# Attention with gated experts on one core: weighted sums in pairs, row statistics issued by POOL, and a context chunk ahead of the third stack loads

## Chip, cores and metric

One core of a Trainium2 chip (trn2) runs the whole program. The metric is device time in microseconds (us), median of the runs, lower is better. Engines: PE is TensorE, ACT ScalarE, DVE VectorE, POOL GpSimd, SP SyncE, which here only issues DMAs.

## What is computed

x is 8 x 512 x 256 float32, the context 8 x 1601 x 256. Cross-attention with 16 heads of 16 channels and a gated residual come first, then a feed-forward over 8 experts of which each token takes two. The softmax of the attention runs over the queries (axis 2 of head, query, key), so each key row is normalised on its own:

```python
def _L0_xattn_ref(q, k, v, Wq, Wk, Wv, Wo):
    scale = Dm ** (-0.5)
    qh, kh, vh = heads(q @ Wq.T), heads(k @ Wk.T), heads(v @ Wv.T)
    attn = jnp.einsum('bhnc,bhlc->bhnl', qh * scale, kh)
    attn = jax.nn.softmax(attn, axis=2)
    attn = attn / jnp.sum(attn, axis=-1, keepdims=True)
    out = jnp.einsum('bhnl,bhlc->bhnc', attn, vh)
    return out @ Wo.T

x = x + jnp.tanh(g_xattn[0]) * _L0_xattn_ref(_layernorm(x), ctx_1024, ctx_1024, Wq, Wk, Wv, Wo)
x = x + jnp.tanh(g_ffn[0]) * _L0_ffn_ref(_layernorm(x), router_w, w1, w2)   # 8 experts, top 2, exact gelu
```

## The kernel before, in words

**The attention loop.** The 8 batches follow one another, each in 52 steps: 4 groups of 4 heads, by 13 tiles of 128 key rows (12 whole ones, and a 13th of the 64 rows that are left; the single last key row is handled apart, as "lone" row). A step is: scores of the tile for the 4 heads, in two units of two heads each (`unit_scores`, PE, two matmuls of 128x512, L822); for each unit the negated maximum over the queries (DVE, L1247); exp with the sum as a by-product, one activation per head (ACT, L1041); the reciprocal of the sums (DVE, L1231); the value rows scaled by it (POOL, `weigh_values`, L1469); and, LAG = 3 steps later, the weighted sum of the tile into the accumulator `acc` (`weigh`, PE, L849: 8 matmul records, four of them side by side in 32 columns each). The lone row's sum (L855) hangs behind the `weigh` of one step in each group (steps 12, 15, 34 and 47 in batches 1 to 7; 12, 25, 38 and 51 in batch 0).

**Two rings.** Scores live in 3 PSUM slots, one a unit. The matmul of head j of unit u waits for the activation of the same head of unit u - 3 (L821). So the first unit of step s+1 waits for the second unit of step s-1. Probabilities live in a ring of 4 steps: ACT's first activation of step s waits for `weigh` of step s-4 (L1038).

**Side work.** `FILL_AT` gives single steps a "fill" of the one bank `spare`: the projections of the next batch (k in 8 pieces, q in 2, v in 7), turns (transposes) of the outputs of this batch, and the output projection, logits and prefix sums of the batch before. A k, q or v piece (not the last v) and an output projection are halved: the first half on PE in the step before, the second in its own step (`Iteration.halves`). ACT takes a k or q piece at the start of its step (L983), DVE the residual (L1134), POOL two more bf16 parts (L1533 and, a step later, L1525), and SP stores the parts to DRAM (`store_parts`, L502). From there SP loads them as the stacks of the next batch (`load_stacks`, 16 DMAs a group, L459 and L464).

**PE's order** is written out in `run` of the tensor block (L859 to L879). In a plain step: first unit, fill, second unit, then `weigh` of step s-3. Where `begins_behind(s)` holds (a first half or a turn begins in s, and s-1 had a fill too, and step s-3 isn't the first of its group), `weigh` of s-3 comes right behind the first unit instead.

**Row statistics of the next batch.** DVE makes mean and variance by step 16 (L1280), POOL the reciprocal deviation in step 17 (`one_over_deviation`, L1439 and L1441). SP then writes both to DRAM as 2 x 512 single float32 (`spread_x_stats`, L514), waits for that to land (L518), and reads them back onto all partitions (`gather_x_stats`, L519). POOL uses them in steps 24 to 27 (L1514, L1518). In batch 0 these two stand in SP's order before the stores of k pieces 3 and 4, in the others behind the store of piece 4.

**Context.** `load_ctx` (L526, L531) loads the context of batch b+2 in 4 column chunks at the end of an iteration, behind the stack loads of groups 1 and 2; chunk c waits for the v piece that reads its columns last. Piece 0 of k in the next iteration, whose first half is in step 0, reads chunk 0 (L740).

After the last batch come routing and 71 blocks of expert work, which the change leaves alone.

Of the kernel before, what the change touches and what calls it, by code (L numbers as in the profile page):

```python
# [33 lines left out]
P = 128  # L34
# [7 lines left out]
KC = D // P  # L42
# [18 lines left out]
KCHUNK = 4  # L61
# [91 lines left out]
SHIFT_X = 24  # L153


class Iteration:
# [32 lines left out]
    def begins_behind(self, s):  # L189

        begun = any(halves == (0,) or f[0] in TURNS for f, halves in self.halves(s))
        return begun and self.fill(s - 1) is not None and (s - LAG) % GROUP_STEPS > 0
# [62 lines left out]
def attention_and_routing(nc, ctx, block, keep, x, x_t_in, ctx_t, g_xattn, g_ffn, wq_t, wk_t, wv_t, wo_t, router_t,  # L255
# [236 lines left out]
    def _(sp):  # L492
# [17 lines left out]
        def spread_x_stats(it):  # L510
            b = it.b
            sp.wait_ge(rstd_step, 2 * (b + 2))
            for s, stat in ((0, mv1[:, :, 0]), (1, rstd1[:, 1, :])):
                sp.dma_start(x_stats_dram[s].rearrange("(t p) -> p t", p=P), stat, allow_slow_non_contiguous=True).then_inc(x_stats_stored, 16)  # L514

        def gather_x_stats(it):
            b = it.b
            wait_apart(sp, x_stats_stored, 32 * (b + 1), passed_sp)  # L518
            sp.dma_start(x_stats[:, :, :], x_stats_dram.partition_broadcast(P)).then_inc(x_stats_in, 16)  # L519

# [5 lines left out]
        def load_ctx(it):  # L526

            for c in range(KCHUNK):
# [29 lines left out]
        def run(it):  # L558
# [13 lines left out]
            if it.next:  # L572
# [3 lines left out]
                for c in ORDER[0:KCHUNK]:  # L576
                    if b == 0 and c == KC + 3:
                        spread_x_stats(it)
                    store_parts(it, c)
# [3 lines left out]
            if it.next:  # L583
                for c in ORDER[KCHUNK:2 * KCHUNK]:
                    if b == 0 and c == KC + 4:
                        gather_x_stats(it)
                    store_parts(it, c)
                    if b > 0 and c == KC + 4:
                        spread_x_stats(it)
                        gather_x_stats(it)  # L590
# [10 lines left out]
            if it.next:  # L601
# [11 lines left out]
                for g in range(1, G - 1):  # L613
                    sp.wait_ge(scores_ready, units_by_group(b, g + 1))
                    load_stacks(b + 1, g)
            if it.ahead:
                load_ctx(it)
# [40 lines left out]
    def _(pe):  # L658
# [200 lines left out]
        def run(it):  # L859
            for s in range(STEPS):  # L860
                late = s >= LAG and it.cur and it.begins_behind(s)
                if it.cur:
                    unit_scores(it.b, s, 0)
                if late:
                    weigh(it.b, s - LAG)
                    if not it.fill(s):
                        unit_scores(it.b, s, 1)
                for f, halves in it.halves(s):
                    fill(it, *f, halves)
                if late and it.fill(s):  # L870
                    unit_scores(it.b, s, 1)
                if it.tail and s == LOGITS - 1:
                    first_logits(it)
                if it.cur and not late:
                    unit_scores(it.b, s, 1)
                    if s >= LAG:
                        weigh(it.b, s - LAG)
# [961 lines left out]
```

## Time and profile before

| | us |
|---|---|
| median of 3 runs (lowest to highest) | 1807.41 (1803.83 to 1809.83) |
| the profiled execution's own time | 1806.2 |
| its span, first to last instruction | 1804.5 |
| mean granted TensorE clock | 0.994 of full speed |

The profiled execution lies 1.2 us below the median; between its span and its own time lie 1.7 us. In the rows below a line is: start (us from the span's start), duration, engine (PEld is PE's weight load, SPq and POOLq a DMA queue), line of the kernel, operation, output tile <- input tiles, shapes, number of records merged into the row, and in brackets how long the engine had been idle before it and who ended that. A row of the waits is: who waited for whom, us in total, times, longest. w_all is the tile that holds stacks, context and probabilities, room holds x, attention output and statistics. An iteration's work on all five engines runs side by side, so an idle time counts only where nothing else covers it.

### The profile page before, as it was taken

How to read it: one execution, taken by the hardware profiler on the slowest of the kernel's cores; microseconds unless marked ns; L12 is line 12 of the kernel's file. 1: busy time of each engine (PE TensorE's matmuls, PEld its weight loads, DVE VectorE, ACT ScalarE, POOL GpSimd, SP SyncE). 2: the span in 40 equal slices, each digit the busy share in tenths (PEclk: the TensorE clock that was granted, in tenths of full speed). 3: DMA queues.
4: the chain of work that ended last, by engine and by line, in shares of the span. 5: the costliest groups of instructions: out<-in, count | busy, mean ns of one | idle time of the engine just before them, and what ended most of it. 6: DMA issues, size and time to landing. Idle time of an engine off the chain costs nothing.

```text
span 1804.5 us, 32470 instructions
## 1 busy us (share of the span) xinstructions
PE 1706.4 (95%) x10342; PEld 925.6 (51%) x10466; DVE 1399.6 (78%) x2320; ACT 1250.0 (69%) x3521; POOL 550.6 (31%) x830
## 2 busy tenths in 40 slices
PE   8989899999999999999999999889899999999997
PEld 5223333333333333333233333225899999999997
DVE  7978899999899999999989999997344444444442
ACT  5989899999999999999999999996111111111111
POOL 3231153343234234334323522213222222222222
PEclk9999999999999999999999999999999999999999
DMA  8638514712821651481282154319322222222221
GB/s 227 151 61 204 131 49 123 211 40 67 227 71 52 180 152 45 123 215 41 66 222 77 47 147 121 137 71 270 117 38 35 38 35 35 38 35 38 35 36 29
DMA packets 144265, 182.12 MB, mean 101 GB/s; under 512 B 22448, under 2 KB 120880, under 8 KB 144144
## 3 DMA queue, kind: packets, MB, share of 16 engines
q1 hardware_dynamic: 129168, 159.67, 33.2%
q0 software_dynamic: 14144, 20.47, 6.5%
q8 instruction: 57, 0.93, 0.2%
q14 instruction: 64, 0.52, 0.1%
q10 hardware_dynamic: 832, 0.53, 0.1%
HBM read 126.69 MB, written 53.91 MB: 100 GB/s over the span
## 4 chain that ended last, share of the span: by engine, by line
PE 49%; DVE 26%; issue 9%; ACT 9%; DMA 3%; POOL 2%; SPq 2%; POOLq 0%; DVEq 0%; ACTq 0%
DVE negmax L1247 18%; PE scores L1651 14%; PE scores L1664 13%; ACT w_all L1041 8%; PE acc L849 7%; PE scores L822 6%; PE spare L686 3%; SPq L464 1%; DVE resid L1134 1%; PE acc L855 1%; DVE rz L1231 1%; DMA routed<-routed_rows,place 1%; PE spare L1641 1%; PE spare L672 1%; DVE o_acc L1237 1%
## 5 line engine op out<-in xcount | busy, mean ns | idle before, releaser
L1041 ACT ACTIVATE w_all<-scores,negmax 128x512 f32<-128x512 f32 x1600 | 1086.2, 749 | 57.1 <-DVE negmax L1247 53.1
L1247 DVE TENSOR_REDUCE negmax<-scores 128x2 f32<-128x1024 f32 x809 | 967.6, 1206 | 55.7 <-PE scores L822 47.0
L822 PE MATMUL scores<-q_stack,w_all 128*128 128x512 bf16 x1412 | 455.4, 384 | 54.5 <-ACT w_all L1041 37.7
L849 PE MATMUL acc<-w_all,vz 128*32 128x512 f32 x3328 | 443.7, 605 | 0.2
L1041 ACT ACTIVATION_READ_ACCUMULATOR w_all<-scores,negmax 128x1 f32 x1600 | 429.0, 268 | 0.0
L1697 ACT ACTIVATE projections<-scores 128x512 f32<-128x512 f32 x142 | 84.8, 597 | 446.8 <-PE scores L1651 441.7
L822 PEld LDWEIGHTS scores<-q_stack,w_all 128*128 128x128 bf16 x1536 | 129.3, 98 | 515.4 <-ACT w_all L1041 443.2
L1469 POOL TENSOR_TENSOR vz<-w_all,rz 128x68 f32<-128x68 f32 x416 | 124.7, 300 | 768.6 <-DVE rz L1231 728.2
L1651 PEld LDWEIGHTS scores<-row_t,q_stack 128*128 128x128 f32 x2272 | 264.5, 192 | 6.1 <-DVE row_t L1724 1.5
L1651 PE MATMUL scores<-row_t,q_stack 128*128 128x128 f32 x2272 | 265.6, 275 | 1.1 <-DVE row_t L1724 1.0
L1664 PE MATMUL scores<-room,projections 128*128 128x256 f32 x1136 | 256.8, 379 | 0.0
L1777 POOL DMA_INDIRECT out<-row_t,gate_token x71 | 118.7, 1671 | 410.8 <-DVE row_t L1737 376.9
L1664 PEld LDWEIGHTS scores<-room,projections 128*128 128x128 f32 x1136 | 210.4, 190 | 25.7
L1730 DVE COPY gate_token<-parts 128x2 f32<-128x2 f32 x71 | 12.0, 170 | 184.1 <-DMA out<-row_t,gate_token 184.1
L849 PEld LDWEIGHTS acc<-w_all,vz 128*32 128x32 f32 x3328 | 66.8, 108 | 136.9 <-issue 120.6
L1737 DVE TENSOR_SCALAR row_t<-scores,gate_token 128x256 f32<-128x256 f32 x71 | 34.4, 484 | 96.5 <-PE scores L1664 96.4
L672 PE MATMUL spare<-w_all,projections 128*128 128x409 f32 (+1 forms) x228 | 98.5, 515 | 7.2 <-DMA w_all<-in_ctx_t 3.8
L686 PE MATMUL spare<-projections,w_all 128*128 128x256 f32 x400 | 104.5, 384 | 0.3 <-ACT w_all L968 0.2
L1714 DVE COPY q_stack<-w_all 128x2048 f32 x71 | 87.0, 1226 | 1.5 <-issue 1.5
L1719 DVE COPY room<-w_all 128x2048 f32 x71 | 86.4, 1217 | 0.0
L686 PEld LDWEIGHTS spare<-projections,w_all 128*128 128x128 f32 x400 | 75.8, 192 | 16.7 <-issue 3.5
L1231 DVE RECIPROCAL rz<-z 128x4 f32<-128x4 f32 x416 | 69.8, 168 | 6.3 <-ACT w_all L1041 6.3
(231 smaller groups left out, 1162.1 us busy)
## 6 DMA issues: line engine op xcount, KB each, us to landing
w_all<-k_parts SPq DMA_DIRECT2D x248, 204.4 KB, 3.7
w_all<-in_w SPq DMA_DIRECT2D x16, 1024.0 KB, 10.2
q_stack<-q_parts SPq DMA_DIRECT2D x248, 64.0 KB, 3.5
k_parts<-parts SPq DMA_DIRECT2D x42, 306.8 KB, 3.4
w_all<-in_ctx_t SPq DMA_DIRECT2D x24, 409.0 KB, 6.5
parts<-routed SPq DMA_DIRECT2D x71, 129.0 KB
q_parts<-parts SPq DMA_DIRECT2D x14, 384.0 KB, 3.9
routed<-pad_row SPq DMA_DIRECT2D x8, 645.0 KB
```

The lines of the kernel that those rows point to most:

```text
L672: mm = pe.matmul(bank[:, 0:KCOLS[c + 1] - KCOLS[c]], wk_sb[:, k, m * P:(m + 1) * P], ctx_sb[:, k, KCOLS[c]:KCOLS[c + 1]], start=(k == 0), ...
L686: mm = pe.matmul(bank[:, cols], rows, wv_sb[:, k, :], start=(k == 0), stop=(k == KC - 1))
L822: mm = pe.matmul(scores[:, bank + j % 2, :], k_stacks[g][:, j, lt * P:(lt + 1) * P], q_stack[:, g, j, :], start=True, stop=True)
L849: mm = pe.matmul(acc[32 * j:32 * j + 32, :], vz[:, s % RING, j, :], probs[:, s % RING, j if lt < LT else j // 2, :], start=(lt == 0), stop ...
L1041: act.activation(lone_probs[:, :] if alone else probs[:, s % RING, j, :], scores[:, 2 * (u % SLOTS) + j % 2, :], ACT.Exp, bias=negmax[:, u ...
L1231: dve.reciprocal(into, sums).then_inc(rz_ready, 1)
L1247: dve.tensor_reduce(negmax[:, u % 4, 0:n], scores[:, 2 * (u % SLOTS):2 * (u % SLOTS) + n, :], AX.X, ALU.max, negate=True).then_inc(negmax_ ...
L1469: pool.tensor_tensor(vz[:, s % RING, :, 0:DH + 1], v_ones[b % 2][:, lt, g * GH:(g + 1) * GH, :], rz[:, s % RING, :].unsqueeze(2).to_broadc ...
L1651: mm = pe.matmul(ps_hidden[:, slot * BANKS + h // HB, (h % HB) * BLK:(h % HB + 1) * BLK], w1_sb[:, slot, k * HID + h * P:k * HID + (h + 1) ...
L1664: mm = pe.matmul(ps_y[:, slot, 0:D], hidden[:, slot, h * BLK:(h + 1) * BLK], w2_sb[:, slot, h * D:(h + 1) * D], start=(h == 0), stop=(h == ...
L1714: dve.tensor_copy(w1_sb[:, slot, :], w1_all[:, bass.ds(e * (KC * HID), KC * HID)]).then_inc(w1_ready, 1)
L1777: pool.indirect_dma_start(out=out, out_offset=bass.IndirectOffsetOnAxis(gate_token[:, slot, 1:2].bitcast(U32), 0), in_=result[:, slot, :], ...
```

## The change

PE's order comes from a plan made per iteration (`weighed`). A `weigh` that would stand at the end of a step is put off where the next step has its own `weigh` behind the first unit: then both stand there, back to back. SP no longer issues the statistics: POOL issues the two stores in step 17, and in step 22 it waits for them and issues the read. The first context chunk is issued behind the stack loads of group 1, ahead of those of group 2.

```diff
--- before.py
+++ after.py
@@ -150,7 +150,7 @@
 OUT = 9
 STATS_X = (7, 11, 12, 13)
 CENTRE_X = 17
-SHIFT_X = 24
+SPREAD_X, SHIFT_X = 22, 24
 
 
 class Iteration:
@@ -189,7 +189,21 @@
     def begins_behind(self, s):
 
         begun = any(halves == (0,) or f[0] in TURNS for f, halves in self.halves(s))
-        return begun and self.fill(s - 1) is not None and (s - LAG) % GROUP_STEPS > 0
+        return begun and self.fill(s - 1) is not None
+
+    def weighed(self):
+
+        plan, following = [], 0
+        for s in range(STEPS):
+            due = s - LAG
+            behind, at_end = range(0), range(0)
+            if following <= due:
+                if self.begins_behind(s) and due % GROUP_STEPS > 0:
+                    behind, following = range(following, due + 1), due + 1
+                elif not (s + 1 < STEPS and self.begins_behind(s + 1) and (due + 1) % GROUP_STEPS > 0):
+                    at_end, following = range(following, due + 1), due + 1
+            plan.append((behind, at_end))
+        return plan
 
     def chunk(self, name, i):
 
@@ -507,25 +521,14 @@
                 load_q_block(sp, stack_in[g], b, g, blk)
                 load_k_block(sp, stack_in[g], b, g, blk)
 
-        def spread_x_stats(it):
-            b = it.b
-            sp.wait_ge(rstd_step, 2 * (b + 2))
-            for s, stat in ((0, mv1[:, :, 0]), (1, rstd1[:, 1, :])):
-                sp.dma_start(x_stats_dram[s].rearrange("(t p) -> p t", p=P), stat, allow_slow_non_contiguous=True).then_inc(x_stats_stored, 16)
-
-        def gather_x_stats(it):
-            b = it.b
-            wait_apart(sp, x_stats_stored, 32 * (b + 1), passed_sp)
-            sp.dma_start(x_stats[:, :, :], x_stats_dram.partition_broadcast(P)).then_inc(x_stats_in, 16)
-
         def load_x(it):
 
             sp.wait_ge(xn_ready, 2 * (it.b + 2))
             sp.dma_start(x_in[:, :, :], x_rows[it.b + 2]).then_inc(x_loaded, 16)
 
-        def load_ctx(it):
-
-            for c in range(KCHUNK):
+        def load_ctx(it, chunks):
+
+            for c in chunks:
                 cols = slice(KCOLS[c], KCOLS[c + 1])
                 sp.wait_ge(fill_taken, it.made("v", last_v_of(c)))
                 sp.dma_start(ctx_sb[:, :, cols], ctx_rows[it.b + 2][:, :, cols]).then_inc(ctx_in[c], 16)
@@ -574,20 +577,13 @@
                 for g in range(G):
                     wait(sp, stack_in[g], stacks_by(b, g))
                 for c in ORDER[0:KCHUNK]:
-                    if b == 0 and c == KC + 3:
-                        spread_x_stats(it)
                     store_parts(it, c)
             if it.tail:
                 sp.wait_ge(fill_taken, it.made("out_proj", 1))
                 sp.dma_start(out_rows[b - 1], x2[:, :, :]).then_inc(x2_stored, 16)
             if it.next:
                 for c in ORDER[KCHUNK:2 * KCHUNK]:
-                    if b == 0 and c == KC + 4:
-                        gather_x_stats(it)
                     store_parts(it, c)
-                    if b > 0 and c == KC + 4:
-                        spread_x_stats(it)
-                        gather_x_stats(it)
             if b == 0:
                 load_stacks(0, 3)
             if it.cur:
@@ -613,8 +609,10 @@
                 for g in range(1, G - 1):
                     sp.wait_ge(scores_ready, units_by_group(b, g + 1))
                     load_stacks(b + 1, g)
+                    if g == 1 and it.ahead:
+                        load_ctx(it, range(1))
             if it.ahead:
-                load_ctx(it)
+                load_ctx(it, range(1, KCHUNK))
 
         def load_w1_behind(group):
 
@@ -857,24 +855,21 @@
             mm.then_inc(pv_done, 1)
 
         def run(it):
-            for s in range(STEPS):
-                late = s >= LAG and it.cur and it.begins_behind(s)
+            for s, (behind, at_end) in enumerate(it.weighed()):
                 if it.cur:
                     unit_scores(it.b, s, 0)
-                if late:
-                    weigh(it.b, s - LAG)
-                    if not it.fill(s):
-                        unit_scores(it.b, s, 1)
+                for step in behind:
+                    weigh(it.b, step)
+                if behind and not it.fill(s):
+                    unit_scores(it.b, s, 1)
                 for f, halves in it.halves(s):
                     fill(it, *f, halves)
-                if late and it.fill(s):
-                    unit_scores(it.b, s, 1)
                 if it.tail and s == LOGITS - 1:
                     first_logits(it)
-                if it.cur and not late:
+                if not (behind and not it.fill(s)):
                     unit_scores(it.b, s, 1)
-                    if s >= LAG:
-                        weigh(it.b, s - LAG)
+                for step in at_end:
+                    weigh(it.b, step)
                 if s < LAG and it.tail:
                     weigh(it.b - 1, STEPS + s - LAG)
 
@@ -1506,6 +1501,12 @@
                 if it.next and s == CENTRE_X:
                     wait_apart(pool, mv_ready, (b + 2) * NT, passed_pool)
                     one_over_deviation(mv1, rstd1, rstd_step, (b + 1) * 2)
+                    for i, stat in ((0, mv1[:, :, 0]), (1, rstd1[:, 1, :])):
+                        pool.dma_start(x_stats_dram[i].rearrange("(t p) -> p t", p=P), stat,
+                                       allow_slow_non_contiguous=True).then_inc(x_stats_stored, 16)
+                if it.next and s == SPREAD_X:
+                    wait_apart(pool, x_stats_stored, 32 * (b + 1), passed_pool)
+                    pool.dma_start(x_stats[:, :, :], x_stats_dram.partition_broadcast(P)).then_inc(x_stats_in, 16)
                 if it.next and s in (SHIFT_X, SHIFT_X + 1):
                     k = s - SHIFT_X
                     if k == 0:
```

## Rows read from the trace of the kernel before

**Rows 1.** Page, busy time of each engine over the span.
```profile
PE 1706.4 (95%) x10342; PEld 925.6 (51%) x10466; DVE 1399.6 (78%) x2320; ACT 1250.0 (69%) x3521; POOL 550.6 (31%) x830
```

**Rows 2.** Timeline of batch 3, steps 13 to 15, engines PE, ACT and DVE.
```profile
536.16 0.38 PE L822 MATMUL scores<-q_stack,w_all 128*128 128x512 bf16 x1
536.47 1.06 PE L849 MATMUL acc<-w_all,vz 128*32 128x512 f32 x8
536.52 0.68 ACT L1041 ACTIVATE w_all<-scores,negmax 128x512 f32<-128x512 f32 x1
537.47 0.61 PE L822 MATMUL scores<-q_stack,w_all 128*128 128x512 bf16 x2
538.01 1.06 PE L849 MATMUL acc<-w_all,vz 128*32 128x512 f32 x8
538.89 1.04 PE L855 MATMUL acc<-lone_probs,lone_vz 128*17 128x512 f32 x8
539.86 0.61 PE L822 MATMUL scores<-q_stack,w_all 128*128 128x512 bf16 x2
...
540.51 1.22 DVE L1247 TENSOR_REDUCE negmax<-scores 128x2 f32<-128x1024 f32 x1 [0.63 <-PE scores L822]
541.77 0.69 ACT L1041 ACTIVATE w_all<-scores,negmax 128x512 f32<-128x512 f32 x1
```

**Rows 3.** Timeline of batch 3, steps 45 and 46, ACT and PE.
```profile
629.54 0.87 ACT L1041 ACTIVATE w_all<-scores,negmax 128x512 f32<-128x512 f32 x1
...
630.56 0.39 PE L822 MATMUL scores<-q_stack,w_all 128*128 128x512 bf16 x1 [0.24 <-ACT w_all L1041]
```

**Rows 4.** Timeline of batch 3, steps 35 to 37, ACT and PE.
```profile
602.77 0.83 ACT L1041 ACTIVATE w_all<-scores,negmax 128x512 f32<-128x512 f32 x1
...
606.12 0.66 PE L754 MATMUL spare<-ident,room 128*128 128x128 f32 x4
...
608.75 0.69 ACT L1041 ACTIVATE w_all<-scores,negmax 128x512 f32<-128x512 f32 x1 [0.56 <-DVE negmax L1247]
```

**Rows 5.** Timeline of batch 3, steps 6 to 8, ACT and PE.
```profile
516.41 0.71 ACT L1041 ACTIVATE w_all<-scores,negmax 128x512 f32<-128x512 f32 x1
...
518.78 0.61 PE L822 MATMUL scores<-q_stack,w_all 128*128 128x512 bf16 x2
```

**Rows 6.** Timeline, end of batch 0 to step 0 of batch 1, SP and PE.
```profile
185.17 2.12 SPq L531 DMA_DIRECT2D w_all<-in_ctx_t  x4
...
190.51 0.58 PE L672 MATMUL spare<-w_all,projections 128*128 128x408 f32 x1 [3.81 <-DMA w_all<-in_ctx_t]
```

**Rows 7.** Timeline, ACT: first activation and take of k piece 2, batches 1 and 3.
```profile
188.74 0.69 ACT L1041 ACTIVATE w_all<-scores,negmax 128x512 f32<-128x512 f32 x1
...
225.82 0.58 ACT L983 ACTIVATE parts<-spare 128x409 bf16<-128x409 f32 x1
...
497.06 0.69 ACT L1041 ACTIVATE w_all<-scores,negmax 128x512 f32<-128x512 f32 x1
...
528.02 0.58 ACT L983 ACTIVATE parts<-spare 128x409 bf16<-128x409 f32 x1
```

**Rows 8.** Waits of the SP queue: the stores of the statistics.
```profile
SPq L231 <- DMA x_stats<-rstd: 70.5, 7, 12.4
```

**Rows 9.** Timeline of batch 0, steps 17 to 24, POOL, SP and ACT.
```profile
85.58 0.96 POOL L1525 TENSOR_TENSOR parts<-resid,parts 128x409 bf16<-128x409 f32 x1
...
92.72 0.36 SPq L502 DMA_DIRECT2D k_parts<-parts  x1
...
103.63 0.52 ACT L983 ACTIVATE parts<-spare 128x409 bf16<-128x409 f32 x1 [4.26 <-DMA k_parts<-parts]
...
111.02 0.69 ACT L1041 ACTIVATE w_all<-scores,negmax 128x512 f32<-128x512 f32 x1 [2.87 <-DVE negmax L1247]
```

**Rows 10.** Stores of k parts in 60 to 130 us: landing times, minimum, median, maximum.
```profile
DMA to landing us min/median/max: 3.1/3.9/10.8
```

**Rows 11.** Timeline, start of the run, POOL issuing eight loads.
```profile
22.90 4.11 POOL L459 DMA_DIRECT2D q_stack<-q_parts  x8 [3.02 <-DMA q_parts<-w_all]
```

## The prediction

> **What bounds the kernel now.** I read the page first. PE is busy 95% of the span and DVE 78% [rows 1], but these are averages over two stages, and the change touches only the attention loop, so I went on to its timeline. There a step holds four activations on ACT, two maxima of 1.22 us on DVE [rows 2], and two units of scores, a weighted sum of about 1 us and the side work on PE. The three engines run at nearly the same rate, so the question in each step is whose chain ends last. Steps 13 to 15 of batch 3 show it [rows 2]: DVE stood idle for 0.63 us until the second unit of step 15 (539.86) was there, and ACT could begin that unit only at 541.77. PE spent the time before on two weighted sums and the lone row's. In step 37 ACT idles 0.56 us in the same way [rows 4]. Batches 2 to 6 repeat the pattern.
>
> Two stalls stand outside this rhythm. In batch 1, step 0, PE waits 3.81 us for the context's first chunk [rows 6]. In batch 0, step 23, ACT waits 4.26 us for a store of k parts, which landed 10.8 us after its issue at 92.72, where the median is 3.9 [rows 9, 10]; a wait of 2.87 us follows in step 25. In front of that store SP had issued the statistics, 2 KB a piece in single floats, which took up to 12.4 us to land [rows 8].
>
> **Part 1, weighted sums in pairs.** The plan makes 16 pairs in each of batches 1 to 6, 14 in batch 0 and 3 in batch 7, 113 in all. What a pair saves can be read: from one weighted sum to the scores behind it PE needs 1.00 us (536.47 to 537.47), to the lone row's sum behind it, which has the same column form, only 0.88 (538.01 to 538.89). Into a weighted sum it is 0.31 us from the last scores matmul (536.16 to 536.47), while a scores matmul takes 0.23 where nothing changes (537.47 to 538.01 for two, less the 0.31). So a pair saves about 0.12 + 0.08 = 0.20 us of PE [rows 2].
>
> What it costs is a cover. The first unit of step s+1 needs the slot that ACT's second unit of step s-1 leaves. Before, a weighted sum stood between, and hid that wait. Now PE waits with both sums still to do, and the second unit of step s+1 stands behind them. The latency from an activation's end to the matmul that waited for it is 629.54 + 0.87 = 630.41 to 630.56, so 0.15 us [rows 3]. With that each pair can be worked out.
>
> Steps 14/15: the slot's last activation ends at 536.52 + 0.68 = 537.20, so the second matmul of the unit starts at 537.35. Then 0.31 into the first sum, 0.88 to the second, 0.88 to the lone row's, 0.97 out of it (538.89 to 539.86): second unit at 540.39 instead of 539.86, 0.53 later [rows 2]. DVE was waiting for it, so all of it reaches ACT.
>
> Steps 36/37: 602.77 + 0.83 + 0.15 = 603.75, then 0.31 + 0.88 + 0.88 + 0.97 gives the turn at 606.79 instead of 606.12, 0.67 later, and ACT, idle there, follows [rows 4]. Steps 49/50 have the same pattern, also with a lone row and a turn: 0.66.
>
> Steps 7/8: 516.41 + 0.71 + 0.15 = 517.27, then 0.31 + 0.88 + 1.00 gives 519.46 instead of 518.78, 0.68 later [rows 5]. DVE is not idle here, its own queue covers about half. Steps 3/4 and 9/10 are alike; I take 0.27 for each of the three. Steps 21/22 and 39/40 give 0.15 each. In the stretch of v pieces (steps 43 to 48), of q pieces and at 27/28 the delays fit under ACT, which is never idle there: nothing, as long as ACT's queue is full; without that cover each would cost 0.3.
>
> A steady batch: 0.53 + 0.67 + 0.66 + 0.8 + 0.3 = 2.96 us, six of them 17.8. Batch 0, with one lone row in a pair, I put at 1.2, batch 7 at 0.6. Sum +19.6. Bounds: all 113 pairs on the path and no slot wait save 0.20 x 113 = 23; the 68 pairs outside the stretch of v, with 0.68 each, would cost 46. I stay by the pairs worked out one by one.
>
> Here a rule speaks for the change. The Trainium skill, "TensorEngine Tiling (Array Packing)", Key Properties, says that changing the tiling mode drains TensorE. The 0.12 and 0.08 us of [rows 2] agree with it. By that rule alone the pairs would be worth the 23 us of the bound.
>
> **Part 2, context chunk 0.** It moves ahead of 16 DMAs. SP needs 2.12 us for four, 0.53 each, so it goes out 8.5 us sooner, about 176.7 instead of 185.17, and with the 5.3 us that it took (185.17 to 190.51) it lands at 182. PE began to wait at 190.51 - 3.81 = 186.70 [rows 6]. In other batches it was in time. Worth: from ACT's first activation to the take of k piece 2, batch 1 needs 225.82 - 188.74 = 37.08 us, batch 3 528.02 - 497.06 = 30.96 [rows 7]. The difference, 6.1 us, holds the wait and what the slower PE clock behind it cost. Late next is chunk 1, out at about 185.7 and landing at 191. It is needed two steps after chunk 0, and a step is 30.96 / 11 = 2.8 us [rows 7], so at 192.3; a wait of 1 us at most. Group 2's loads and the last chunks go out 0.5 us later and have a group's time. So -6.1, between -3.8 and -6.5.
>
> **Part 3, the statistics.** SP is free of them, POOL gets three DMAs. Eight loads cost POOL 4.11 us [rows 11], 0.5 each; stores in single floats may take 1. In step 17 POOL's low part of the piece before stands behind them, and the value rows of step 17, which have two steps of slack. In step 22 POOL waits for the landing. Five steps of 2.8 us are 14 us, the landing took up to 12.4 [rows 8], with POOL's issue added about 14 too. If it is late by 1 or 2 us, what stands behind it are value rows that PE needs three steps on: nothing. If that cover were gone, each such us would count in seven batches.
>
> Batch 0 is another matter. The low part of k piece 2, at 85.58 now [rows 9], moves to about 87.5, its store to 88.5, which is behind the statistics and no longer before them. ACT takes piece 4, which needs that store landed, two steps before it came to piece 5 (103.63 - 4.26 = 99.4), at about 93.8. If single-float writes hold up what is written after them, as they held piece 3's store for 10.8 us, the stall of 4.26 and most of the 2.87, say 6.6 us together, goes, and one of about the same size comes two steps sooner. If POOL's queue is apart, all 6.6 us go. Bounds: -6.6 and +5. I take 0, by the row that is nearest, the store that was held.
>
> The Trainium skill, "Trainium Kernel Development and Optimization", Key Constraints, says that DMAs of SP, ACT and POOL run on the same 16 DMA engines and that another issuing engine saves only issue time. By it the hold-up stays, and the sum is the one I give.
>
> **Sum**, on the profiled execution's own time: 1806.2 + 19.6 - 6.1 + 0 = 1819.7, that is 1820. The median is 1.2 above that execution; I leave it there. What a measurement of this kernel can tell from no change is about 0.3%, 5.4 us.
>
> **Rivals.**
> A. *Not slower: the late second units are absorbed.* Place: steps 3 to 15, 36/37, 49/50. DVE's queue or ACT's hides them, or the first unit, which is now up to 0.4 us sooner, gives the time back. For it: DVE and ACT are busy nearly all the time. Against: the idle times of 0.63 and 0.56 us stand exactly behind these units. It decides if the two sums end within 0.3 us of their old place. Time: 1806.2 - 6.1 = 1800, or 1794 if the statistics' stall goes too. Chance 0.17.
> B. *Faster: PE's column form is the bound.* Of 16 pairs 9 lie where PE is late; 57 x 0.20 = 11 us: 1806 - 6 - 11 = 1789. Against: the slot wait above. Chance 0.06.
> C. *As forecast, but POOL's queue is apart*: 1820 - 6.6 = 1813. Chance 0.20.
> D. *The new hold-up is longer than the old*: piece 2's store lands at 103, ACT waits 9 us and loses some 2 behind it, where 6.6 were lost: 1824. Chance 0.15.
> My forecast, 1820, has 0.42, its own range 1813 to 1827.
>
> **How the numbers follow.** Faster (under 1802): B and over half of A, 0.16. Same (to 1812.8): the rest of A, nearly half of C, a little of the forecast, 0.21. Slower: 0.63. The range 1799 to 1829 leaves out B, the low end of A and the high end of D.
>
> **What would show it.** Part 1: in step 15 of batch 3 the two sums in a row and the second unit 0.5 us later against ACT's activations, PE's waits for ACT at L822 grown, and a steady batch 3 us longer. Part 2: no wait for in_ctx_t, and 31 us from first activation to piece 2 in batch 1. Part 3: ACT's wait for k_parts in batch 0 gone, or moved to piece 4. I am wrong if steady batches are not longer than now.

## The result: 1.25% slower, and the profile after

| | before | changed |
|---|---|---|
| median (lowest to highest) | 1805.62 (1802.64 to 1809.83), 4 runs | 1828.76 (1824.76 to 1830.42), 4 runs |
| profiled execution, its span | 1806.2, 1804.5 | 1824.76, 1823.0 |

The ratio is 1.0125, 95% interval 1.0108 to 1.0143, that is +22.6 us (19.5 to 25.8). The forecast was 1820, slower: the sign held, the size was short, and the median lies 0.24 us inside the upper end of the range, 1829, and outside the forecast's own 1813 to 1827. Below, the page after: the busy line, the chain's shares by engine, and four of the costliest groups (busy, mean ns | idle before it, and who ended it).

```profile
PE 1692.1 (93%) x10347; PEld 946.7 (52%) x10466; DVE 1397.9 (77%) x2320; ACT 1254.4 (69%) x3521; POOL 568.9 (31%) x851
...
PE 41%; DVE 25%; ACT 24%; issue 7%; DMA 1%; POOL 1%; SPq 0%; DVEq 0%; POOLq 0%; ACTq 0%
...
L1036 ACT ACTIVATE w_all<-scores,negmax 128x512 f32<-128x512 f32 x1600 | 1085.8, 737 | 70.9 <-DVE negmax L1242 67.6
L1242 DVE TENSOR_REDUCE negmax<-scores 128x2 f32<-128x1024 f32 x809 | 968.7, 1207 | 66.3 <-PE scores L820 56.0
L820 PE MATMUL scores<-q_stack,w_all 128*128 128x512 bf16 x1417 | 454.5, 384 | 99.4 <-ACT w_all L1036 85.6
L847 PE MATMUL acc<-w_all,vz 128*32 128x512 f32 x3328 | 419.4, 601 | 0.4 <-POOL vz L1464 0.4
```

PE is busy 14 us less than before [rows 1] and the kernel is longer. The weighted sums alone (L847, before L849) went from 443.7 to 419.4 us. So the saving in PE's work was real: 24.3 us on the sums, where 113 pairs at the 0.20 us of [rows 2] make 23. But PE's wait for ACT in front of the scores grew from 37.7 to 85.6 us, DVE's wait for scores from 47.0 to 56.0, and ACT's for DVE from 53.1 to 67.6. The engine got idler, which is what a lost cover looks like.

The same place as [rows 2], steps 14 and 15 of batch 3, in the timeline after:

```profile
541.12 0.68 ACT L1036 ACTIVATE w_all<-scores,negmax 128x512 f32<-128x512 f32 x1
...
541.94 0.39 PE L820 MATMUL scores<-q_stack,w_all 128*128 128x512 bf16 x1 [0.28 <-ACT w_all L1036]
542.26 1.92 PE L847 MATMUL acc<-w_all,vz 128*32 128x512 f32 x16
544.00 1.04 PE L853 MATMUL acc<-lone_probs,lone_vz 128*17 128x512 f32 x8
544.98 0.61 PE L820 MATMUL scores<-q_stack,w_all 128*128 128x512 bf16 x2
...
545.62 1.23 DVE L1242 TENSOR_REDUCE negmax<-scores 128x2 f32<-128x1024 f32 x1 [1.15 <-PE scores L820]
...
546.88 0.69 ACT L1036 ACTIVATE w_all<-scores,negmax 128x512 f32<-128x512 f32 x1 [0.57 <-DVE negmax L1242]
```

The slot's last activation ends at 541.80 and the matmul that waited starts at 541.94. Then come both sums in one record of 16, the lone row's, and the second unit 3.18 us after the slot was free (544.98 - 541.80). Before it was 2.66 (539.86 - 537.20): 0.52 more, where the forecast had 0.53. DVE's idle time before that unit grew from 0.63 to 1.15. Steps 36/37 likewise, to set beside [rows 4], where ACT idled 0.56:

```profile
609.31 0.39 PE L820 MATMUL scores<-q_stack,w_all 128*128 128x512 bf16 x1 [0.26 <-ACT w_all L1036]
609.63 1.92 PE L847 MATMUL acc<-w_all,vz 128*32 128x512 f32 x16
611.37 1.04 PE L853 MATMUL acc<-lone_probs,lone_vz 128*17 128x512 f32 x8
612.35 0.66 PE L752 MATMUL spare<-ident,room 128*128 128x128 f32 x4
...
614.97 0.69 ACT L1036 ACTIVATE w_all<-scores,negmax 128x512 f32<-128x512 f32 x1 [1.21 <-DVE negmax L1242]
```

A batch's length is read from ACT's first activation in it to the first of the next. For batch 3, before it is the first of [rows 7] for batch 3 and the line below:

```profile
648.16 0.69 ACT L1041 ACTIVATE w_all<-scores,negmax 128x512 f32<-128x512 f32 x1
```

that is 151.10; after:

```profile
500.79 0.69 ACT L1036 ACTIVATE w_all<-scores,negmax 128x512 f32<-128x512 f32 x1
...
655.18 0.69 ACT L1036 ACTIVATE w_all<-scores,negmax 128x512 f32<-128x512 f32 x1
```

154.39. Read in this way for every step, the first activation of a step is later, against the kernel before, by 0.23 more from step 5 on, 0.39 from 10, 0.21 from 12, 0.50 from 16, 0.19 from 23, 0.23 from 25, 0.65 from 38, 0.14 from 41 and 0.61 from 51. I call these "jumps" below; they add up to 3.15, and the other 0.14 of the 3.29 lies in shifts of under 0.1 us each. Batches 3 to 6 all have them (in batch 4 0.21 of the last comes at step 49 already). The others: batch 0 157.41 to 159.31, batch 1 157.22 to 154.88, batch 2 151.11 to 155.30, with 0.9 more than its neighbours at step 23, and batch 7, read to the start of its last step, 137.04 to 139.12.

The other two parts of the change, batch 0 on POOL and ACT, then the turn of the batch on SP:

```profile
85.18 0.85 POOL L1505 DMA_DIRECT2D x_stats<-mv  x1 [0.29 <-POOL rstd L1436]
86.02 0.77 POOL L1505 DMA_DIRECT2D x_stats<-rstd  x1
86.81 0.98 POOL L1526 TENSOR_TENSOR parts<-resid,parts 128x409 bf16<-128x409 f32 x1
...
99.39 0.51 ACT L978 ACTIVATE parts<-spare 128x408 bf16<-128x408 f32 x1 [6.38 <-DMA k_parts<-parts]
...
175.14 0.58 SPq L534 DMA_DIRECT2D w_all<-in_ctx_t  x1
...
186.74 1.61 SPq L534 DMA_DIRECT2D w_all<-in_ctx_t  x3
```

ACT's wait of 4.26 us before piece 5 [rows 9] is now one of 6.38 before piece 4, for the store of piece 2, whose low part (86.81) now follows the single-float stores. The context's chunk 0 goes out at 175.14 instead of 185.17, and no wait for it is left at the start of batch 1.

### The profile page after: what moved, and what is told of

Its sections match the earlier page's. It is cut to its first block, busy times and chain, and to the rows that moved or that the text cites. A ratio compares the mean times of both kernels' runs of the same rounds, so it can differ in the third digit from the quotient of the medians.

```text
span 1823.0 us, 32468 instructions
## 1 busy us (share of the span) xinstructions
PE 1692.1 (93%) x10347; PEld 946.7 (52%) x10466; DVE 1397.9 (77%) x2320; ACT 1254.4 (69%) x3521; POOL 568.9 (31%) x851
## 4 chain that ended last, share of the span: by engine, by line
PE 41%; DVE 25%; ACT 24%; issue 7%; DMA 1%; POOL 1%; SPq 0%; DVEq 0%; POOLq 0%; ACTq 0%
ACT w_all L1036 23%; DVE negmax L1242 17%; PE scores L1652 14%; PE scores L1665 13%; PE acc L847 5%; PE scores L820 3%; PE spare L684 2%; PE acc L853 1%; DVE resid L1129 1%; PE spare L1642 1%; DVE rz L1226 1%; DVE room L1137 1%; DMA k_parts<-parts 1%; DVE o_acc L1232 1%; ACT w_all L985 1%
## 5 line engine op out<-in xcount | busy, mean ns | idle before, releaser
L1036 ACT ACTIVATE w_all<-scores,negmax 128x512 f32<-128x512 f32 x1600 | 1085.8, 737 | 70.9 <-DVE negmax L1242 67.6
L820 PE MATMUL scores<-q_stack,w_all 128*128 128x512 bf16 x1417 | 454.5, 384 | 99.4 <-ACT w_all L1036 85.6
L847 PE MATMUL acc<-w_all,vz 128*32 128x512 f32 x3328 | 419.4, 601 | 0.4 <-POOL vz L1464 0.4
L1036 ACT ACTIVATION_READ_ACCUMULATOR w_all<-scores,negmax 128x1 f32 x1600 | 409.2, 256 | 0.0
L820 PEld LDWEIGHTS scores<-q_stack,w_all 128*128 128x128 bf16 x1536 | 135.0, 98 | 497.7 <-ACT w_all L1036 395.6
L847 PEld LDWEIGHTS acc<-w_all,vz 128*32 128x32 f32 x3328 | 78.1, 108 | 157.4 <-issue 141.5
```

Of the source, the lines that this page charges most:

```text
L820: mm = pe.matmul(scores[:, bank + j % 2, :], k_stacks[g][:, j, lt * P:(lt + 1) * P], q_stack[:, g, j, :], start=True, stop=True)
L847: mm = pe.matmul(acc[32 * j:32 * j + 32, :], vz[:, s % RING, j, :], probs[:, s % RING, j if lt < LT else j // 2, :], start=(lt == 0), stop ...
L1036: act.activation(lone_probs[:, :] if alone else probs[:, s % RING, j, :], scores[:, 2 * (u % SLOTS) + j % 2, :], ACT.Exp, bias=negmax[:, u ...
```

## Experiments

All are edits of the kernel before; the diffs for pairs below are shown against the change's plan. The differences in us are the ratio and its interval times the median of the kernel before on the same chip (1803.57, 1800.47 and 1798.99 in the three sets).

**The three parts alone.** Theory 1 is that of the forecast; rival 2 blames POOL, rival 3 the order of loads. The packing alone takes `weighed`, `begins_behind` and `run` from the change's diff, `e_ctx` its `load_ctx` hunks, `e_stats` its statistics hunks.

> Kernel before with the pairs of weighted sums alone (16 in each of batches 1 to 6, 14 in batch 0, 3 in batch 7); SP still issues the statistics and the context's chunks stand where they were. Theory 1 (a pair takes away the weighted sum that covered the wait for a scores slot, and puts two sums in front of the next second unit): a steady batch is 3.3 us longer, 154.4 instead of 151.1, with the steps at the end of 14/15, 36/37 and 49/50 carrying some 0.5 to 0.65 each; batch 1 also 3.3 longer, batch 7 2.1; in all +23 us, 1829. Rival 2 (pairs cost nothing or save their 0.20 us each; the steady batches got longer because POOL issues the statistics, whose DMAs hold POOL up or slow DVE beside it): steady batches at 151.1 or 148, time 1783 to 1806. Rival 3 (the order of the context's chunks): same as rival 2 for this run.

1826.02, ratio 1.0129 (1.0112 to 1.0147): +23.3 us (20.2 to 26.5). Batch 3 154.4, the same jumps to 0.1 us, batch 7 +1.97. Batch 1 missed what I had put down, 0.25 us longer (157.47) and not 3.3: PE waited 3.04 us for the context there and not 3.81, and its mean granted clock over 185 to 197 us was 1.00, in the kernel before 0.86. Rivals 2 and 3 fall: all that the steady batches lost comes from the pairs.

> Kernel before with the context's first chunk ahead of the third stack loads alone. Theory 1: only the wait at the start of batch 1 goes and the slow PE clock behind it: batch 1 is 5.6 us shorter, 157.2 to 151.6, all other batches as before within 0.3 us; 1800. Rival 3 (the chunk pushes the loads of stacks behind it, and something waits for them): steady batches longer by up to 3 us, 1806 to 1820.

1798.46, ratio 0.9975 (0.9963 to 0.9987): -4.5 us (-6.7 to -2.3). Batch 1 took 152.01; batches 2 to 7 are as before but for 0.5 us once. A gain that the whole change hides.

> Kernel before with the row statistics issued by POOL alone. Theory 1: steady batches 151.1 as before; batch 0 1.5 us longer, because the stores in single floats now go out ahead of k piece 2's store and ACT waits some 6.4 us for it before piece 4, where it had waited 4.3 us for piece 3's store before piece 5 and 2.9 behind; 1805 to 1808. Rival 2 (POOL's issue and wait are what lengthened the steady batches): steady batches 154, 1825. Rival 4 (POOL's queue is apart from SP's and the held store goes): ACT waits nowhere for a store of k parts in batch 0, 1799.

1807.69, ratio 1.0024 (1.0014 to 1.0033): +4.3 us (2.5 to 5.9), more than I expected. Batches 3 to 7 are as before; batches 1 and 2 were 1.3 and 1.0 us longer in this profile. In batch 1 the granted clock over 185 to 197 us was lower, 0.72 against 0.86. Batch 2's is in the changed kernel too (its 0.9 at step 23), and did not come with POOL's stores in another place (below); its cause is not shown. In batch 0:

```profile
99.26 0.51 ACT L965 ACTIVATE parts<-spare 128x408 bf16<-128x408 f32 x1 [6.74 <-DMA k_parts<-parts]
```

Why +4.3 and not +1.5: in the profiled execution of before, batch 0 took 157.4 us. Of the seven kernels of this study that leave the statistics with SP in their old place, six took 153.0 to 154.6 there (`e_pack` 156.9), and all waited 1.4 to 2.9 us before piece 5, not 4.26. With POOL's stores ahead the wait was 6.7 and, with all three parts, 6.4, batch 0 157.4 and 159.3. Part of such a stall is the clock: PE, short of work behind ACT, was busy for 10.9 of the 16 us from 96 to 112 in the kernel before and for 13.7 in `e_ahead`, and its mean granted clock there, a mix of the levels of 2.4 and 1.2 GHz, was 0.79 in the first and 1.00 in the second. It was 0.79 in all four kernels with a batch 0 above 156 us (before, changed, `e_pack`, `e_stats`) and 0.89 or 1.00 in the seven others with the stores of the statistics in step 17 (batch 0 at 153.0 to 154.6). The execution that I read had a long stall.

The parts add up: 23.3 - 4.5 + 4.3 = 23.1, against 22.6 for the whole.

**Which pairs.** The condition for putting a sum off gets a tuple of the steps in which a pair may end:

```diff
-                elif not (s + 1 < STEPS and self.begins_behind(s + 1) and (due + 1) % GROUP_STEPS > 0):
+                elif not (s + 1 in PAIRED and self.begins_behind(s + 1) and (due + 1) % GROUP_STEPS > 0):
```

> Kernel before with only those 8 pairs of a batch that end in steps 17, 28, 30, 33, 35, 44, 46 and 48, where the changed kernel's steps were not longer (ACT has a k, q or other side piece and is the last to end); the other weighted sums stand where they stood before. Theory 1: nothing lengthens there because ACT's queue covers the late second unit, and nothing shortens because PE is not the last: steady batches 151.1 within 0.3, time 1805 within 2 us. Rival 5 (each pair costs the same wherever it stands, the steps of the changed kernel only show it late): half of 3.3, that is 1.6 us a steady batch, 1816. Rival 6 (each pair saves 0.20 us of PE and this shows where nothing stands against it): 1.6 us a batch shorter, 1794.

1811.19, ratio 1.0034 (1.0020 to 1.0047): +6.1 us (3.6 to 8.5). Neither theory 1 nor 5 nor 6: two jumps of 0.47 at step 38 and 0.44 at 51, and nothing that all batches share in the stretches themselves. So the row of the forecast that said "nothing" for these pairs is wrong, and the bill comes later. In this profile batches 2 to 4 lost a further 1.33 us in step 30, of which more in the last section.

> Kernel before with only the three pairs of a batch that end in steps 15, 37 and 50 (those with a lone row's sum, a turn, or both behind them); 2 a batch in batch 0, none in batch 7. Theory 1 (each pair's delay is its own: slot wait plus two sums ahead of the second unit): the jumps are where they were with all pairs, 0.50 at step 16, 0.65 at 38, 0.61 at 51, so a steady batch is 1.8 us longer, 152.9; 1804 + 12 = 1816. Theory 1b (the eight pairs that I held for covered already give 0.47 at step 38 and 0.44 at step 51, so PE falls behind within the stretch and ACT's queue only puts the bill off; the three pairs then add little to it): 0.50 at 16, and only 0.2 at 38 and 51 each, 0.9 a batch, 1810. Rival (what the eight pairs cost is a slower PE clock only): as theory 1.

1812.16, ratio 1.0069 (1.0055 to 1.0082): +12.4 us (9.9 to 14.8). Jumps of 0.51, 0.67 and 0.66 at steps 16, 38 and 51. The forecast had worked out 0.53, 0.67 and 0.66 from the rows of before. But the eight others give 0.47 and 0.44 without them, and all sixteen no more than 0.65 and 0.61: at these places the costs do not add up, the larger one counts.

> Kernel before with two pairs a batch only, the ones that end in steps 35 and 48: the last of the eight before ACT's queue runs empty in steps 37 and 50. With eight pairs the steps 38 and 51 were 0.47 and 0.44 us longer. If only the last pair counts (each slot wait sets PE back to the same distance behind ACT, and nothing adds up): 0.47 and 0.44 again, a steady batch 152.0. If the pairs add up under ACT's queue: 0.1 to 0.2 at each, a steady batch 151.4. Rival, as I forecast it (covered, nothing): 151.1.

1804.36, ratio 1.0035 (1.0023 to 1.0047): +6.3 us (4.1 to 8.5), jumps 0.48 and 0.44, all of what eight pairs gave. Its timeline, batch 3, steps 36 and 37 (PE, then ACT):

```profile
597.67 0.59 PE L838 MATMUL scores<-q_stack,w_all 128*128 128x512 bf16 x2
598.10 1.03 PE L702 MATMUL spare<-projections,w_all 128*128 128x256 f32 x4
598.97 0.59 PE L838 MATMUL scores<-q_stack,w_all 128*128 128x512 bf16 x2
599.49 1.06 PE L865 MATMUL acc<-w_all,vz 128*32 128x512 f32 x8
600.49 0.60 PE L838 MATMUL scores<-q_stack,w_all 128*128 128x512 bf16 x2
601.02 1.06 PE L865 MATMUL acc<-w_all,vz 128*32 128x512 f32 x8
601.91 1.04 PE L871 MATMUL acc<-lone_probs,lone_vz 128*17 128x512 f32 x8
602.88 0.66 PE L770 MATMUL spare<-ident,room 128*128 128x128 f32 x4
...
605.51 0.69 ACT L1054 ACTIVATE w_all<-scores,negmax 128x512 f32<-128x512 f32 x1 [1.04 <-DVE negmax L1260]
```

No PE line has an idle time in brackets: behind the pair of steps 34/35 PE works without a break to the turn of step 37, so it has nowhere to make up what the slot wait cost. ACT's full queue hid that for two steps; when it ran dry, ACT idled 1.04 us instead of the 0.56 of [rows 4], 0.48 more. Two pairs cost there what eight did, so what the pairs before them lose does not add up. My reading, which no row shows by itself: each slot wait puts PE back to the same distance behind ACT, so only the last pair before such a place counts.

**Where the sums stand.** All pairs again, with another order inside them. `e_between` puts the second unit between the two sums:

```diff
-                for step in behind:
+                for step in behind[0:1]:
                     weigh(it.b, step)
...
-                for step in at_end:
+                for step in (*behind[1:], *at_end):
```

> All pairs of the plan, but the second unit of scores stands between the two sums: unit 0, the sum put off, unit 1, side work, the other sum at the end of the step. So the slot wait of the first unit is uncovered as in the changed kernel, but one sum only stands ahead of the second unit, and no two sums are back to back. If theory 1's larger part is the two sums ahead of the second unit: DVE gets that unit about 0.9 us sooner than in the changed kernel, 0.5 sooner than before, the jumps at 16, 38 and 51 go or turn into gains, a steady batch takes 150.5 to 151.5, 1797 to 1806. If the larger part is PE's lost time at the uncovered slot wait (0.3 to 0.5 us a pair that nothing gives back): a steady batch stays at 153.5 to 154.5, 1820 to 1827.

1822.76, ratio 1.0117 (1.0102 to 1.0132): +21.1 us (18.4 to 23.8), a steady batch 154.71. The gains of 0.30 and 0.22 at steps 38 and 51 are there, and jumps elsewhere eat them: 0.44 at 16, 0.91 at 19, 0.58 at 25. The second unit comes early, at 543.65 in step 15, but with the slot wait in front of it and one sum still to do PE is late one or two steps on. The batch came out 0.2 us above the 153.5 to 154.5 put down for the uncovered wait and far from the 150.5 to 151.5 for the other reading, so the larger part is the uncovered wait.

`e_ahead` gives both sums to the end of the step before:

```diff
-                elif not (s + 1 < STEPS and self.begins_behind(s + 1) and (due + 1) % GROUP_STEPS > 0):
-                    at_end, following = range(following, due + 1), due + 1
+                else:
+                    n = 2 if s + 1 < STEPS and self.begins_behind(s + 1) and (due + 1) % GROUP_STEPS > 0 else 1
+                    at_end, following = range(due, due + n), due + n
```

In `run` the second unit stays where the kernel before has it: `early` sends it right behind the first in steps that begin a half.

> All pairs of the plan, but both sums stand at the end of the step before, not behind the first unit: the second sum is taken a step early instead of the first a step late. Two sums are still back to back, so PE saves what a pair saves, and they stand where PE has a slot wait to come, which they cover. Theory 1: no uncovered slot wait and no two sums ahead of the second unit; the first unit comes 0.9 us later and the second as before less 0.2; a steady batch of 150 to 152.5, 1794 to 1812, the saving showing where PE was late (steps 15, 37, 50). Rival 2 (two sums in a row as such are what costs, by the accumulator or the weight loads behind each other): 154 as in the changed kernel, 1826.

1817.18, ratio 1.0088 (1.0074 to 1.0102): +15.8 us (13.3 to 18.4), a steady batch 153.64. It missed both my intervals, 150 to 152.5 for the batch and 1794 to 1812 for the time. The slot wait is covered, but now the first unit of the next step stands behind both sums:

```profile
538.66 1.92 PE L864 MATMUL acc<-w_all,vz 128*32 128x512 f32 x16
540.40 1.04 PE L870 MATMUL acc<-lone_probs,lone_vz 128*17 128x512 f32 x8
541.38 1.04 PE L837 MATMUL scores<-q_stack,w_all 128*128 128x512 bf16 x4
...
542.02 2.35 DVE L1260 TENSOR_REDUCE negmax<-scores 128x2 f32<-128x1024 f32 x2 [1.09 <-PE scores L837]
```

One unit is 1.2 us of work for DVE, two sums are 1.9 us of PE. The rival, that two sums in a row cost as such, has the rows against it: 1.92 us for both, where one alone takes 1.06. In each of the three orders tried for a pair some unit is late, another one each time; one sum to a step, as before, was the shortest of the four.

**What held the store.** `e_stats_behind` moves POOL's two stores below the block that makes the low part of the piece before, in the same step 17.

> Kernel before with POOL issuing the statistics, but in step 17 behind the low part of the piece before, so that k piece 2's store goes out beside the first of them and not behind both. If it is the place of the single-float stores ahead of a k store that costs (4 us over the kernel before, ACT waiting 6.7 us before piece 4): the wait before piece 4 goes or is under 2 us, one of 2 to 4 us before piece 5 is there as in the kernel before, 1803 within 2. If it is the issuing engine (POOL's own queue): as with the statistics by POOL, 1808, and the wait of 6.7 us stays before piece 4. If the store of piece 2 is slowed as well by what starts beside it: a wait of 3 to 6 us before piece 4, 1805 to 1808.

1797.31, ratio 0.9994 (0.9984 to 1.0004): no difference to the kernel before. The wait before piece 4 is gone, the old one before piece 5 is back:

```profile
100.03 0.52 ACT L965 ACTIVATE parts<-spare 128x409 bf16<-128x409 f32 x1 [1.75 <-DMA k_parts<-parts]
```

POOL issues in both, so the issuing engine is not it; what counts is which store of k comes next behind the single floats.

**Better versions.** `e_best1` has the context's chunk ahead, SP keeps the statistics, and batch 0 makes them earlier:

```diff
+FIRST_STATS_X = (7, 8, 9, 10)
+FIRST_CENTRE_X = 11
...
-                    if b == 0 and c == KC + 3:
+                    if b == 0 and c == KC:
                         spread_x_stats(it)
+                    if b == 0 and c == KC + 2:
+                        gather_x_stats(it)
...
```

> Kernel before with the context's first chunk ahead, and in batch 0 alone the statistics of the next batch made in steps 7 to 10 instead of 7 to 13 and finished in 11, so that SP stores them ahead of k piece 0's store, where the pieces stand three steps apart, and reads them back ahead of k piece 2's. If single-float stores hold up the store behind them and this is all that the two waits of ACT in batch 0 were (4.3 and 2.9 us): both waits go, batch 0 is 6 us shorter than now, and with the context's 4.6 it gives 1793. Rival (the wait comes from the pieces standing close together in steps 14 to 23, whatever stands between the stores): 1799, as the context chunk alone. Rival (the hold-up goes to k piece 0's store and ACT waits before piece 2): 1797.

1790.51, ratio 0.9947 (0.9933 to 0.9961): -9.5 us (-12.1 to -7.0), faster than both kernels. Batch 0 149.28, batch 1 152.03, the rest as before. The two stores now go out at 66.22 and 66.63, and piece 0's store behind them is held as the others were, 9.0 us:

```profile
66.22 0.37 SPq L516 DMA_DIRECT2D x_stats<-mv  x1
66.63 0.51 SPq L516 DMA_DIRECT2D x_stats<-rstd  x1
...
DMA to landing us min/median/max: 3.1/3.5/9.0
```

ACT waits nowhere for it, since piece 2 is taken five steps after piece 0. The hold-up is much the same (10.8 us before); it costs nothing there. And the granted clock over 96 to 112 us was 1.00.

`e_best2` and `e_best3` try steps 37 and 50 alone on top of it. `e_best2` puts `PAIRED = (37, 50)` into the order of `e_between`; `e_best3` pairs nothing, and in these two steps leaves the step's own sum, with the lone row's, to the end of the step:

```diff
-        return begun and self.fill(s - 1) is not None and (s - LAG) % GROUP_STEPS > 0
+        return begun and self.fill(s - 1) is not None and (s - LAG) % GROUP_STEPS > 0 and s not in (37, 50)
```

> The fastest kernel so far (context's first chunk ahead, statistics of batch 0 early) with, in steps 37 and 50 alone, the weighed sum of the step before put off to behind unit 0, unit 1 behind the turn, and the own sum (with the lone row's) at the end of the step. With all pairs in this order the steps 38 and 51 were 0.30 and 0.22 us shorter. Theory 1 (the sums ahead of the second unit are what ACT waits for in these steps): 0.3 to 0.5 us a batch at each of the two, 4 to 7 us in all, 1784 to 1787. Rival (PE's lost time at the slot wait takes it back in the steps behind): 1790 within 2.

> As the fastest so far, with steps 37 and 50 in the plain order: unit 0, turn, unit 1, then the own sum and the lone row's; no sum is put off, so the slot wait stays covered by the sum at the end of step 36 or 49. Theory 1: ACT gets the second unit 1 to 1.9 us sooner, its wait of 0.56 us there goes, and what the later sum costs shows only if the turn or the ring of probabilities (ACT's first activation of step s needs the sum of step s-4) comes too late: a gain of up to 0.6 a step, 1782 to 1788. Rival (the first units of steps 38 and 51 stand behind both sums now and are late instead): 1790 to 1796.

`e_best2` 1790.16, ratio 0.9947 (0.9934 to 0.9961), nothing over `e_best1`, as the rival of this run had it: 0.34 us a batch gained at the two places, and given back in other steps. `e_best3` 1788.24, ratio 0.9937 (0.9924 to 0.9951), its five runs (1788.09 to 1788.74) all below the five of `e_best2` (1789.73 to 1790.76). The best of the study, -11.3 us (-13.7 to -8.8), some 2 us from the order of the two steps: the jumps at 38 and 51 are -0.35 and -0.37, a steady batch is 150.86 against 151.10 before, as 0.48 us come back in other steps. I expected up to 0.6 a step and 1782 to 1788, the rival 1790 to 1796; the time lies just above the first, and what the rival named is there too: DVE, before in [rows 4] late for the second unit of step 37, is now late for the first of step 38:

```profile
594.70 1.22 DVE L1251 TENSOR_REDUCE negmax<-scores 128x2 f32<-128x1024 f32 x1 [0.76 <-PE scores L832]
```

## Why the prediction was right, and where its terms were off

**The mechanism held.** What decided the sign was the cover: a sum taken from in front of a slot wait and put behind it. Steps 14/15, 36/37 and 49/50 were worked out at 0.53, 0.67 and 0.66 us; alone on the chip they cost 0.51, 0.67 and 0.66. Steps 3/4, 7/8 and 9/10 were put at 0.81 together and came to 0.83 (jumps at 5, 10 and 12 of 0.23, 0.39 and 0.21). These three pairs, and those of 21/22 and 39/40, were never tried alone: what they cost is read off by place in the kernels with all pairs. Rival B, with the 23 us of the drain, falls although the drain was saved: 24.3 us of L847's busy time. "TensorEngine Tiling (Array Packing)" of the Trainium skill, Key Properties, says that a change of tiling mode drains PE, and the trace agrees, with 0.20 us saved by a pair; what the separated sums were covering, it does not say.

**Off in size: 19.6 for the packing, measured 23.3 (20.2 to 26.5).** A steady batch was 2.96 and came to 3.29, 2.0 us in six. Steps 21/22 were 0.15 and came to 0.42 (jumps at 23 and 25). Batch 7 was 0.6 and came to 2.0, since all three of its pairs show in full: 0.66 at step 6, 0.31 and 0.36 at 9 and 10, 0.66 at 19. I had given the terms of 21/22 and batch 7 no working of their own. Two pairs of each batch, 16/17 and 29/30, had no term at all; `e_pairs_covered` holds both, and they showed nothing of their own. And the 68 pairs of the upper bound do not come out of the plan: three pairs in each of seven batches stand in the stretch of v, which leaves 92, and 63 us at 0.68 each. Nothing else was worked out from that bound.

**Wrong: "in the stretch of v pieces and of q pieces the delays fit under ACT: nothing".** Step by step inside the stretch that is so. But the last pair of it costs 0.44 to 0.48 where ACT's queue ends. In the sum it did not show, because steps 36/37 and 49/50 have pairs of their own there and the larger cost alone counts. Had the change made only the covered pairs, my method would have said no change, and it is 0.34% slower.

**Off in size: the context, -6.1, measured -4.5 (-6.7 to -2.3).** Place and direction as forecast: batch 1, no wait for in_ctx_t, and 222.70 - 190.61 = 32.1 us from first activation to piece 2, where I had said 31. So 1.1 of the 6.1 us is there without the wait. The rest was once more read from one execution: in the nine kernels with the chunk in its old place PE waited 2.5 to 3.8 us for it, and the granted clock over 185 to 197 us was 0.86 in most, 0.72 in `e_stats`, but 1.00 in `e_pack` and `e_stats_behind`. Batch 1 of the latter took 154.9 us, not 157.2, beside 152.0 with the chunk ahead: there the move would be worth 2.9 us and not 5.2.

**Wrong value: the statistics, 0, measured +4.3 (2.5 to 5.9).** The move of the wait from piece 5 to piece 4 was forecast, and that POOL's queue is not apart: rival C, with 0.20, falls. "Trainium Kernel Development and Optimization", Key Constraints, of the Trainium skill, has it so, the DMAs of SP, ACT and POOL on the same 16 DMA engines. The traces agree: in `e_stats` the single floats are POOL's, and SP's store of piece 2 behind them, at 87.33, landed after 11.8 us, as SP's own store of piece 3 had after 10.8 in the kernel before. What failed was the price of the stall removed: I took 6.6 us from one execution, in which it was at its longest, and set it against a new one "of about the same size". Rival D had the direction, a new stall longer than the old, but by a wrong step: the new one is no longer than I said, the old one is shorter. With the measured terms on the median of the kernel before, 1805.62 + 23.3 - 4.5 + 4.3 = 1828.7, where 1828.76 was measured. On the profiled execution, 1806.2, they can't be set as they stand, since its own batch 0 had the long stall.

**What was luck.** The range held by 0.24 us. Its upper end stood for most of rival D, whose step was wrong, and not for pairs that cost more than I had worked out, which is where the time went; my own range for the forecast, to 1827, was too narrow by 1.8 us.

## What to carry to other kernels

Work that an engine does between two units of a pipeline with few slots may be the cover of a wait. Before two such pieces are joined to save a switch, put beside each other what the switch costs (here 0.20 us) and how late the unit behind them gets (here 0.5 to 0.7). A full queue downstream hides a late unit only if the engine that is late has idle time before that queue runs dry; look at the end of the stretch, not into it. And price a stall from several executions, or give it the range that they show, with the granted clock behind it: here it was 1.4 to 4.3 us in kernels that do the same there, and the clock over the 16 us around it 0.79 to 1.00.

## What the runs showed of the hardware that I had not expected

**The clock can fall in a busy stretch, and slot waits alone don't explain it.** In the kernel with the eight pairs, batch 3, PE waited 0.49, 0.28, 0.28 and 0.28 us for ACT in front of single scores matmuls, and then two sums took 3.44 us, where a pair takes 1.92. The windows below (stretch, length, busy time of PE, PEld, DVE, ACT, POOL, granted clock, DMA share, GB/s) show a mean granted clock of 0.69 there, a mix of the full 2.4 GHz and the half level of 1.2:

```profile
582.51 0.39 PE L838 MATMUL scores<-q_stack,w_all 128*128 128x512 bf16 x1 [0.28 <-ACT w_all L1054]
582.83 3.44 PE L865 MATMUL acc<-w_all,vz 128*32 128x512 f32 x16
...
580.00:584.00 4.00, 2.68 (x13) 0.76 (x16) 4.00 (x8) 4.00 (x12) 1.22 (x2) 0.89 0.05 19
584.00:588.00 4.00, 3.95 (x23) 1.28 (x20) 2.73 (x8) 3.02 (x10) 1.17 (x2) 0.69 0.19 62
...
886.88:890.88 4.00, 2.67 (x17) 0.80 (x20) 4.00 (x8) 4.00 (x12) 1.22 (x2) 1.00 0.06 19
890.88:894.88 4.00, 3.95 (x26) 1.48 (x20) 3.97 (x11) 3.36 (x11) 1.38 (x3) 1.00 0.20 64
```

The last two lines are the same place in batch 5. The fall cost 1.33 us in step 30 in three of the six batches, 2 to 4. Batches 1, 5 and 6 of the same kernel have the same four waits, to a hundredth or two, and a clock of 1.00, and so has batch 3 of both kernels with all pairs, `e_pack` and the changed one. So the waits alone are not the cause; what is was not found.

**POOL pays more to issue a store of single floats**, 0.85 and 0.77 us against SP's 0.48 and 0.55, and that falls on an engine with other work in the step.
